# A four-layer graph network on one core: softmax sums one unit later, neighbour lists and weight products moved behind layer 0's first units

## The chip, the cores and the metric

The kernel runs on one core of a Trainium2 chip. The metric is the device time of one execution in microseconds. A core has five engines with instruction streams of their own: TensorE (PE; its weight loads are listed as PEld), VectorE (DVE), ScalarE (ACT), GpSimd (POOL) and SyncE (SP), which here only issues DMAs. The engines wait for one another by semaphores, and each runs its stream strictly in the order of the program.

## The reference

Four graph layers over 50,000 nodes with 256 features and 25,000 edges sorted by dst; after each a residual and a layer norm. Cut to what matters:

```python
def L0(x):   # dot-product weights without a maximum, sum over edges
    q, k, v = heads(x @ Wq), heads(x @ Wk), heads(x @ Wv)
    score = exp(clip(sum(k[src] * q[dst], -1) / sqrt(32), -5, 5))
    return segment_sum(v[src] * score, dst) / (segment_sum(score, dst) + 1e-9)
def L1(h):   # GIN
    z = (1 + eps) * h + segment_sum(h[src], dst)
    z = relu(z @ W1 + b1) @ W2 + b2
    return relu(layernorm(z + h) * gamma + beta)
def L2(x):   # GAT, with a self-loop for each node
    h = heads(x @ W); e = leaky_relu(a_src(h)[src] + a_dst(h)[dst])
    m = segment_max(e, dst); ex = exp(e - m[dst])
    alpha = ex / segment_sum(ex, dst)[dst]
    return layernorm(segment_sum(h[src] * alpha, dst) + bias + x) * ln_w + ln_b
def L3(x):   # attention with edge features
    k_j, v_j = (x @ Wk + bk)[src] + edge_attr @ We, (x @ Wv + bv)[src] + edge_attr @ We
    a = softmax over dst of sum(q[dst] * k_j, -1) / sqrt(32)
    return segment_sum(v_j * a, dst) + x @ Ws + bs
for L in (L0, L1, L2, L3):
    x = layernorm(x + L(x))
```

## The kernel before, in words

The nodes are worked in 196 units of 256 (two tiles of 128), the edges in 196 chunks of 128. Six stages run one after the other, each with a stream of its own on each engine: `prepare` (index lists, weights, constants; the first 55 us), `layer0` (to about 1045 us), `nodes1` (to 2470), `nodes2` (to 3610), `edges3` (to 4275) and `nodes3` (to the end).

Inside a stage the order is written by hand. `run_units(total, depth, body)` calls `body(s, at)` for steps s = 0, 1, 2, ..., once for each engine, and `at(lag)` is the unit s − lag, or none. So a job with lag 13 does in step s what belongs to unit s − 13, and the jobs of one step stand in each engine's stream in the order of the text. Steps of different engines are tied by semaphores alone.

**prepare.** SP and ACT load the two index arrays and the weights; DVE casts src and dst (L344, L346), makes three masks (L357 and behind it), a table of first edges (L372) that SP stores and loads again (L302, L304), then the products of weights and attention vectors (`wprod`, `watt`), the split of the biases into bf16 parts (`b3`, `b_sum`, L391) and their cast (L393).

**layer0.** POOL gathers source rows (L586), PE turns them (L627) and multiplies (L642); the messages go to memory and come back by SP (L504) for the sum over a unit's edges (L660). `pairs`, the neighbour lists that nodes1 to nodes3 use, is fetched by SP (L599, L601) in sixteen DMAs, eight of 16×24×256 integers (0.39 MB) and eight of 8×256, before SP's loads of unit 0.

**nodes2.** POOL gathers for each unit the rows of hh_d that its nodes' sources name (L1186, two DMAs a unit) into `near_rows`, a ring of NR = 16 buffers; it waits for the semaphore `weighed`. DVE multiplies them by the shares (`weighted`, L1403) and raises `weighed`. Shares are made for groups of GU = 8 units at once, on tiles of 128×128: scores turned by PE (L1241), maxima on DVE (tops), exp on ACT (L1499), sums on DVE (L1133, L1129, reciprocal L1393, shares L1411), turned back by PE (L1288, L1289) and copied as `own_first` by ACT (L1507). PE sums a unit's own shares into `own_ps` (L1297), DVE multiplies them by the unit's own rows (`own`, L1342), POOL adds the residual (L1193, semaphore `based`), and PE sums weighted rows, bias and own (L1265 to L1267) for the unit. PE's step begins with the transposes of L1250 and L1254. Other rings: `hot` of HOT buffers, `hin` of HR = 5, `xin` of XR = 9, `weighted` and `own` of WR = 4.

The lags that matter: POOL gathers at(0), adds own at(16); PE turns the shares and makes own_ps at(14), sums at(17); DVE maxima at(12), sums at(13), L1342 and L1403 at(15). POOL's body is:

```python
gp.wait_ge(weighed, u - NR + 1)     # unit at(0), then its two gathers
gp.indirect_dma_start(out=near_rows[:, u % NR, h, :], ...)
u = at(16)
gp.wait_ge(own_done, u + 1)         # then the own add of unit at(16)
gp.tensor_tensor(own..., own..., xin..., ALU.add).then_inc(based, 1)
```

**nodes3** has the same softmax without own shares: sums at(12), reciprocal at(13), shares at(14), the shares' transposes at(15) (L1785), product with the messages at(16) (L1718), sum at(18) (L1806); its messages come by SP into 24 buffers, and there are no gathers.

## Time and profile before

| | before |
|---|---|
| median of 3 runs | 5031.09 us |
| their lowest and highest | 5024.81, 5033.5 us |
| the profiled execution's own time | 4998.33 us |
| its span | 4996.6 us |
| busy PE, DVE, ACT, POOL | 91%, 80%, 56%, 50% |
| mean granted TensorE clock | 0.938 |

All rows come from the profiled execution, whose time lies 32.8 us below the median of the runs. A row of an instruction is: start in us, duration, engine, line of the kernel, operation, output<-inputs, shape; in brackets how long the engine stood idle before it and what ended that. A busy share over the whole span is a mean over six stages with limits of their own; each has to be read from its own windows.

### The profile page before, as it was taken

The numbers are of one execution on the slowest core, as the hardware profiler recorded it, in microseconds if no ns is written. First come the engines' busy times: TensorE is split into PE (matmuls) and PEld (weight loads), VectorE is DVE, ScalarE is ACT, GpSimd is POOL, SyncE is SP. The second block draws the span as 40 slices with busy tenths as digits, with TensorE's granted clock in tenths as the row PEclk, the third lists the DMA queues.
The fourth block names the chain that finished last, engine by engine and source line by source line (L and its number), as shares of the span: only waits on it lengthen the run. The fifth ranks groups of instructions, "written<-read, shape, count | busy, mean of one in ns | idle before, by whom it ended". The sixth has DMA issues, their size and how long they took to land. (4 is left out here: it accounts for less than half of the span.)

```text
span 4996.6 us, 90737 instructions
## 1 busy us (share of the span) xinstructions
PE 4563.9 (91%) x21673; PEld 3506.0 (70%) x21722; DVE 3986.5 (80%) x13147; ACT 2805.1 (56%) x6326; POOL 2476.3 (50%) x2462
## 2 busy tenths in 40 slices
PE   4999998779999999999888888888799999699998
PEld 3666664448888888888767777777566666577777
DVE  4777778979999999999859999999855555567666
ACT  1787886545555555555547777777611111366565
POOL 3555551237777777777466666666365554000000
PEclk8999996569999999999979999999899999899999
DMA  6777778954444444444468888787555554677775
GB/s 138 210 225 222 223 223 257 298 187 135 150 152 153 149 148 152 153 153 148 143 184 252 244 244 244 243 243 243 183 172 163 163 164 146 193 228 228 223 228 160
DMA packets 911233, 970.10 MB, mean 194 GB/s; under 512 B 104899, under 2 KB 867258, under 8 KB 910892
## 3 DMA queue, kind: packets, MB, share of 16 engines
q1 hardware_dynamic: 500692, 471.58, 32.9%
q10 hardware_dynamic: 327416, 315.35, 18.6%
q0 software_dynamic: 82784, 179.41, 12.3%
q8 instruction: 119, 1.95, 0.2%
q14 instruction: 222, 1.82, 0.1%
HBM read 654.56 MB, written 363.57 MB: 204 GB/s over the span
## 5 line engine op out<-in xcount | busy, mean ns | idle before, releaser
L1186 POOL DMA_INDIRECT nodes_near_rows<-hh_d,source_row x392 | 394.9, 1007 | 401.3 <-DVE nodes_weighted L1403 292.6
L586 POOL DMA_INDIRECT layer_xg<-in_x,edge_rows x392 | 386.7, 987 | 358.5 <-PE layer_t_ps L627 241.5
L884 POOL DMA_INDIRECT nodes_near_rows<-x_d,nodes_cur x392 | 419.0, 1069 | 238.2 <-POOL nodes_cur L879 170.8
L1542 POOL DMA_INDIRECT edges_xg<-x_d,edge_rows x392 | 372.9, 951 | 264.3 <-PE edges_x_ps L1568 172.6
L485 ACT ACTIVATE nodes_x<-nodes_outer_rows,nodes_outer_shift,nodes_outer_rstd 128x256 f32<-128x256 f32 x784 | 428.0, 597 | 61.1 <-issue 51.4
L1597 ACT ACTIVATE edges_xT<-edges_x_ps 128x512 f32<-128x512 f32 x196 | 117.1, 597 | 524.7 <-PE edges_x_ps L1568 524.7
L1806 PE MATMUL nodes_agg<-w_s,nodes_xT 128*128 128x256 f32 x1568 | 405.5, 381 | 0.0
L1004 PE MATMUL nodes_h_ps<-w_h,nodes_x2T 128*128 128x272 f32 x1568 | 392.2, 393 | 8.1 <-ACT nodes_x2T L1081 8.1
L660 PE MATMUL layer_agg<-layer_msg,layer_hot 128*128 128x264 f32 x784 | 314.2, 540 | 73.5 <-issue 65.7
L642 PE MATMUL layer_kv_ps<-w_kv,layer_xT 128*128 128x512 f32 x784 | 372.3, 597 | 1.0 <-DVE layer_made L751 1.0
L994 PE MATMUL nodes_out_ps<-w_b,nodes_hid 128*128 128x256 f32 x1568 | 371.2, 380 | 1.4 <-DVE nodes_inner_rows L925 0.8
L1014 PE MATMUL nodes_hid_ps<-nodes_zT,w_a 128*128 128x256 f32 x1568 | 370.5, 379 | 0.7 <-ACT nodes_zT L1088 0.7
L1633 DVE TENSOR_TENSOR edges_kv<-edges_kv_ps,edges_e_row 128x512 f32<-128x512 f32 x196 | 135.5, 692 | 295.2 <-PE edges_kv_ps L1584 295.2
L1584 PE MATMUL edges_kv_ps<-w_kv,edges_xT 128*128 128x512 f32 x784 | 368.4, 592 | 2.6
L660 PEld LDWEIGHTS layer_agg<-layer_msg,layer_hot 128*128 128x128 f32 x784 | 191.6, 260 | 219.3 <-issue 191.8
L1004 PEld LDWEIGHTS nodes_h_ps<-w_h,nodes_x2T 128*128 128x128 f32 x1568 | 297.3, 190 | 65.8 <-ACT nodes_x2T L1081 10.0
L899 POOL TENSOR_TENSOR nodes_x2b<-nodes_x,row_L_gnn_ln_b 128x512 f32<-128x512 f32 x196 | 265.8, 1356 | 142.0 <-DMA x_d<-nodes_x2b 131.4
L485 ACT ACTIVATE layer_y<-layer_ln_rows,layer_ln_shift,layer_ln_rstd 128x256 f32<-128x256 f32 x392 | 213.8, 592 | 217.0 <-DVE layer_ln_shift L478 217.0
L1014 PEld LDWEIGHTS nodes_hid_ps<-nodes_zT,w_a 128*128 128x128 f32 x1568 | 297.8, 190 | 46.5 <-ACT nodes_zT L1088 1.1
L1806 PEld LDWEIGHTS nodes_agg<-w_s,nodes_xT 128*128 128x128 f32 x1568 | 284.6, 191 | 31.0
L994 PEld LDWEIGHTS nodes_out_ps<-w_b,nodes_hid 128*128 128x128 f32 x1568 | 282.6, 190 | 32.4 <-issue 1.0
L941 DVE SCALAR_TENSOR_TENSOR nodes_scaled<-nodes_inner_rows,nodes_inner_moments,row_L_gnn_gamma 128x256 f32<-128x256 f32 x392 | 300.8, 806 | 0.0
(223 smaller groups left out, 12341.3 us busy)
## 6 DMA issues: line engine op xcount, KB each, us to landing
nodes_xin<-x_d SPq DMA_DIRECT2D x588, 256.0 KB, 3.8
layer_msg<-msg_d SPq DMA_DIRECT2D x392, 132.0 KB
hh_d<-nodes_hh ACTq DMA_DIRECT2D x196, 264.0 KB, 4.1
nodes_msg<-msg_d SPq DMA_DIRECT2D x392, 132.0 KB, 3.1
x_d<-layer_y ACTq DMA_DIRECT2D x196, 256.0 KB, 3.8
x_d<-nodes_x2b ACTq DMA_DIRECT2D x196, 256.0 KB, 3.5
nodes_hin<-hh_d SPq DMA_DIRECT2D x196, 256.0 KB, 3.9
x_d<-nodes_x ACTq DMA_DIRECT2D x196, 256.0 KB
```

The lines of the kernel that those rows point to most:

```text
L485: last = nc.scalar.activation(to[:, h, :], t["rows"][:, ring(u, 4), h, :], ACT.Identity, bias=t["shift"][:, ring(u, 4), h:h + 1], scale=t[ ...
L586: gp.indirect_dma_start(out=xg[:, c % 8, k, :], out_offset=None, in_=x, in_offset=bass.IndirectOffsetOnAxis(ap=edge_rows[:, c, k:k + 1], a ...
L642: last = nc.tensor.matmul(kv_ps[b][:, :], xT[:, b, 0, i, :], w0_kv[:, i, :], start=i == 0, stop=i == KC - 1)
L660: last = nc.tensor.matmul(agg[u % 2][:, h, 0:D + H], hot[:, u % 4, h, :], msg[:, r, h, :], start=True, stop=True)
L884: gp.indirect_dma_start(out=near_rows[:, r, h, :], out_offset=None, in_=x1_d, in_offset=bass.IndirectOffsetOnAxis(ap=cur[:, r, h:h + 1], a ...
L994: last = nc.tensor.matmul(out_ps[ring(u, 2)][:, h * D:(h + 1) * D], hid[:, ring(u, 2), k, h * P:(h + 1) * P], w1_b[:, k, :], start=k == 0, ...
L1004: last = nc.tensor.matmul(h_ps[:, h, 0:D + 2 * H], x2T[:, ring(u, 2), k, h, :], w2_h[:, k, :], start=k == 0, stop=k == KC - 1)
L1014: last = nc.tensor.matmul(hid_ps[:, m * 2 * P:(m + 1) * 2 * P], w1_a[:, k, m * P:(m + 1) * P], zT[:, ring(u, 2), k, :, :].rearrange("p h n ...
L1186: gp.indirect_dma_start(out=near_rows[:, u % NR, h, :], out_offset=None, in_=hh_d, in_offset=bass.IndirectOffsetOnAxis(ap=source_row[:, 2 ...
L1542: gp.indirect_dma_start(out=xg[:, c % 8, k, :], out_offset=None, in_=x3_d, in_offset=bass.IndirectOffsetOnAxis(ap=edge_rows[:, c, k:k + 1] ...
L1584: last = nc.tensor.matmul(kv_ps[r][:, :], xT[:, b, 0, j, :], w3_kv[:, j, :], start=False, stop=j == KC - 1)
L1806: nc.tensor.matmul(to, xT[:, u % 2, k, h, :], w3_s[:, k, :], start=k == 0, stop=False)
```

## The change

It has four parts.

In prepare, the casts of src stand behind the first mask. The loads of the attention vectors and of the biases (six DMAs), and all products of weights, leave prepare.

In layer0, ACT issues these six loads ahead of its first step, and DVE makes the products in twelve pieces, one a step, in steps U0 + 56 to U0 + 67. The masks of the lists, from step U0 + 6 on before, start at step U0 + 24. SP's sixteen `pairs` fetches stand two by two in units 8 to 15.

In nodes2 the sums stay where the maxima's group is one unit further on: sums at(14), the shares' transposes, own_first and own_ps at(15), L1342 and L1403 at(16), POOL's add at(17), PE's sum at(18), and everything behind it one step later; SP's loads of hin, attr and x move by one with them. HOT goes from 18 to 19. NR, XR, HR and WR stay.

In nodes3 the sums go to at(13), and all behind them one step later.

```diff
@@ prepare, DVE @@
-                for k in (1, 0):
-                    ve.wait_ge(edges_in[k], 48)
-                    nc.vector.tensor_copy(ends_f[:, k, :, :], ends_c[:, k, :, :]).then_inc(cast, 1)
-                for k in (1, 0):
-                    last = nc.vector.tensor_copy(pairs[:, :, :, k], ends_c[:, k, :, :])
-                last.then_inc(paired, 1)
+                ve.wait_ge(edges_in[1], 48)
+                nc.vector.tensor_copy(ends_f[:, 1, :, :], ends_c[:, 1, :, :]).then_inc(cast, 1)
+                nc.vector.tensor_copy(pairs[:, :, :, 1], ends_c[:, 1, :, :])
...
+                    if mask is below_lo:
+                        ve.wait_ge(edges_in[0], 48)
+                        nc.vector.tensor_copy(ends_f[:, 0, :, :], ends_c[:, 0, :, :]).then_inc(cast, 1)
+                        nc.vector.tensor_copy(pairs[:, :, :, 0], ends_c[:, 0, :, :]).then_inc(paired, 1)
@@ layer0 @@
-        MASKS = U0 + 6
+        MASKS, WEIGHTS = U0 + 24, U0 + 56
...
                 for u in range(UNITS):
+                    if 8 <= u < 8 + H:
+                        h = u - 8
+                        sp.wait_ge(lists_out, 16)
+                        sp.dma_start(pairs[h * 2 * GU:(h + 1) * 2 * GU, 0:WHOLE, :],
+                                     windows[0:WHOLE * 2 * GU, :].rearrange("(g w) x -> w g x", w=2 * GU)).then_inc(pairs_in, 16)
+                        sp.dma_start(pairs[h * REST:(h + 1) * REST, WHOLE, :], windows[WHOLE * 2 * GU:TILES, :]).then_inc(pairs_in, 16)
...
+                    if WEIGHTS <= s < WEIGHTS + 12:
+                        weights(s - WEIGHTS)
@@ nodes2 @@
-        NR, HR, XR, WR, HOT, LATER = 16, 5, 9, 4, 18, 12
+        NR, HR, XR, WR, HOT, LATER = 16, 5, 9, 4, 19, 12
...
-                    u = at(16)
+                    u = at(17)
                     if u is not None:
                         gp.wait_ge(own_done, u + 1)
...
```

How the streams stand, at the three places where instructions of different kinds change places:

POOL in nodes2, at the first own add (34 gathers stand ahead of it before, 36 after). Before:

```order
L1186 DMA nodes_near_rows<-hh_d,source_row 128x264
L1186 DMA nodes_near_rows<-hh_d,source_row 128x264 [waits nodes2_weighed]
L1186 DMA nodes_near_rows<-hh_d,source_row 128x264
L1193 TENSOR_TENSOR nodes_own<-nodes_own,nodes_xin 128x512 [waits layer0_made_out1,nodes2_own_done]
L1186 DMA nodes_near_rows<-hh_d,source_row 128x264 [waits nodes2_weighed]
```

and after:

```order
L1201 DMA nodes_near_rows<-hh_d,source_row 128x264 [waits nodes2_weighed]
L1201 DMA nodes_near_rows<-hh_d,source_row 128x264
L1201 DMA nodes_near_rows<-hh_d,source_row 128x264 [waits nodes2_weighed]
L1201 DMA nodes_near_rows<-hh_d,source_row 128x264
L1208 TENSOR_TENSOR nodes_own<-nodes_own,nodes_xin 128x512 [waits layer0_made_out0,nodes2_own_done]
L1201 DMA nodes_near_rows<-hh_d,source_row 128x264 [waits nodes2_weighed]
```

Two units' gathers that wait for `weighed`, instead of one's, stand ahead of the first add; from there on the two alternate unit by unit, as before. (A semaphore named for layer0 is one that nodes2 uses again for xin.)

SP at the start of layer0. `windows` are the lists, xin and msg are unit 0's loads. Before:

```order
L596 DMA windows<-layer_wrow 98x4x256
L599 DMA layer_pairs<-windows 16x24x256
L601 DMA layer_pairs<-windows 8x256
```

```order
L601 DMA layer_pairs<-windows 8x256
L495 DMA layer_xin<-in_x 128x2x256
L418 TENSOR_LOAD first_row
L418 ISA x16
L504 ISA
L504 DMA layer_msg<-msg_d 128x264
```

and after:

```order
L575 DMA windows<-layer_wrow 98x4x256
L467 DMA layer_xin<-in_x 128x2x256
L390 TENSOR_LOAD first_row
L390 ISA x16
L476 ISA
L476 DMA layer_msg<-msg_d 128x264
```

Between the two pieces of before stand the other seven pairs of fetches. After, unit 0's loads follow the lists directly.

DVE in nodes2, where the sums of a group begin (the scan of L1133, L1148 after). Before, behind the step with the maxima:

```order
L1388 TENSOR_TENSOR nodes_score_ps<-nodes_score_ps,nodes_top 128x256
L464 BN_AGGR nodes_inner_moments<-nodes_inner_parts 128x2 x2
L1403 TENSOR_TENSOR nodes_weighted<-nodes_near_rows,nodes_share_ps 128x512
L464 BN_AGGR nodes_outer_moments<-nodes_outer_parts 128x2 x2
L1422 TENSOR_TENSOR nodes_outer_rows<-nodes_agg,nodes_xin 128x512
L474 RECIPROCAL nodes_inner_rstd<-nodes_inner_dev 128x2
L474 RECIPROCAL nodes_outer_rstd<-nodes_outer_dev 128x2
L478 SCALAR_TENSOR_TENSOR nodes_inner_shift<-nodes_inner_moments,nodes_inner_rstd 128x2
L478 SCALAR_TENSOR_TENSOR nodes_outer_shift<-nodes_outer_moments,nodes_outer_rstd 128x2
L1133 SCALAR_TENSOR_TENSOR nodes_score_ps<-go_on,nodes_score_ps 128x128
```

and after:

```order
L430 BN_STATS nodes_outer_parts<-nodes_outer_rows 128x6 x2
L1396 TENSOR_TENSOR nodes_agg<-nodes_agg,row_L_gnn_ln_w 128x512
L436 BN_AGGR nodes_inner_moments<-nodes_inner_parts 128x2 x2
L1418 TENSOR_TENSOR nodes_weighted<-nodes_near_rows,nodes_share_ps 128x512
L436 BN_AGGR nodes_outer_moments<-nodes_outer_parts 128x2 x2
L1437 TENSOR_TENSOR nodes_outer_rows<-nodes_agg,nodes_xin 128x512
L446 RECIPROCAL nodes_inner_rstd<-nodes_inner_dev 128x2
L446 RECIPROCAL nodes_outer_rstd<-nodes_outer_dev 128x2
L450 SCALAR_TENSOR_TENSOR nodes_inner_shift<-nodes_inner_moments,nodes_inner_rstd 128x2
L450 SCALAR_TENSOR_TENSOR nodes_outer_shift<-nodes_outer_moments,nodes_outer_rstd 128x2
L1148 SCALAR_TENSOR_TENSOR nodes_score_ps<-go_on,nodes_score_ps 128x128
```

The step ahead of the sums is a plain one after the change; the maxima stand a step further up.

## Rows read from the trace of the kernel before

**Rows 1.** Windows: us, busy PE, PEld, DVE, ACT, POOL, granted clock, DMA share, GB/s
```profile
560.00:760.00 200.00, 200.00 (x783) 123.38 (x782) 141.70 (x557) 161.22 (x307) 108.43 (x109) 1.00 0.74 222
2800.00:3000.00 200.00, 178.20 (x1036) 150.42 (x1035) 185.19 (x661) 146.21 (x369) 122.59 (x112) 0.95 0.82 250
```
**Rows 2.** Line L1241 (count, ns, first and last start) and the waits, both from 2700 to 3500
```profile
L1241 PE MATMUL nodes_score_ps<-ident,nodes_att_edge x72: 275/275/275, 2728.4 to 3465.6; 128*128 128x128 f32 x72
```
```profile
POOL nodes_near_rows L1186 <- DVE nodes_weighted L1403: 240.7, 116, 4.1
```
**Rows 3.** Timeline of nodes2: the links of the loop
```profile
2552.65 0.59 PE L1297 MATMUL nodes_own_ps<-nodes_own_first,nodes_hot 128*128 128x8 f32 x4
2553.28 0.69 DVE L1342 SCALAR_TENSOR_TENSOR nodes_own<-nodes_own_ps,nodes_hin 128x512 f32<-128x512 f32 x1 [4.52 <-PE nodes_own_ps L1297]
...
2812.50 0.69 DVE L1342 SCALAR_TENSOR_TENSOR nodes_own<-nodes_own_ps,nodes_hin 128x512 f32<-128x512 f32 x1
...
2815.17 0.65 DVE L1403 TENSOR_TENSOR nodes_weighted<-nodes_near_rows,nodes_share_ps 128x512 f32<-128x512 f32 x1
...
2816.62 1.02 POOL L1186 DMA_INDIRECT nodes_near_rows<-hh_d,source_row  x1 [0.72 <-issue]
...
2818.97 1.29 POOL L1193 TENSOR_TENSOR nodes_own<-nodes_own,nodes_xin 128x512 f32<-128x512 f32 x1
2819.56 0.65 DVE L1403 TENSOR_TENSOR nodes_weighted<-nodes_near_rows,nodes_share_ps 128x512 f32<-128x512 f32 x1
...
2821.94 0.60 PE L1265 MATMUL nodes_agg<-nodes_weighted,nodes_hot 128*128 128x256 f32 x2
...
2825.12 0.59 PE L1297 MATMUL nodes_own_ps<-nodes_own_first,nodes_hot 128*128 128x8 f32 x4
```
**Rows 4.** Timeline of nodes2: the step with the sums, and the shares
```profile
2828.89 0.43 DVE L1133 TENSOR_TENSOR_SCAN nodes_score_ps<-go_on,nodes_score_ps 128x128 f32<-128x128 bf16 x1 [1.13 <-ACT nodes_score_ps L1499]
2829.23 0.67 DVE L1342 SCALAR_TENSOR_TENSOR nodes_own<-nodes_own_ps,nodes_hin 128x512 f32<-128x512 f32 x1
...
2833.20 0.65 DVE L1403 TENSOR_TENSOR nodes_weighted<-nodes_near_rows,nodes_share_ps 128x512 f32<-128x512 f32 x1
...
2840.62 0.61 PE L1297 MATMUL nodes_own_ps<-nodes_own_first,nodes_hot 128*128 128x8 f32 x4 [0.65 <-ACT nodes_own_first L1507]
```
**Rows 5.** PE's idle times and the clock behind them, timeline and windows
```profile
2834.02 0.64 PE L1250 MATMUL nodes_work_ps<-ident,nodes_hot 128*128 128x128 f32 x2 [2.61 <-ACT nodes_e_row L1489]
...
2877.32 1.19 PE L1265 MATMUL nodes_agg<-nodes_weighted,nodes_hot 128*128 128x256 f32 x2
...
2882.82 0.31 PE L1288 MATMUL nodes_share_ps<-ident,nodes_share 128*128 128x128 f32 x1
...
4401.23 0.30 PE L1785 MATMUL nodes_share_ps<-ident,nodes_share 128*128 128x128 f32 x1 [1.87 <-DVE nodes_weighted L1718]
```
```profile
4401.00:4403.00 2.00, 1.77 (x11) 1.59 (x12) 1.00 (x5) 0.98 (x3) 0.00 (x0) 1.00 0.58 193
2834.00:2836.00 2.00, 1.94 (x6) 1.32 (x7) 2.00 (x11) 1.12 (x3) 1.05 (x2) 0.53 0.64 219
```
**Rows 6.** Timeline of prepare and of layer0's first units
```profile
15.75 0.29 DVE L344 CAST prepare_ends_f<-prepare_ends_c 98x256 f32<-98x256 int32 x1 [7.22 <-DMA prepare_ends_c<-in_src]
15.96 0.49 DVE L346 COPY prepare_pairs<-prepare_ends_c 98x256 int32<-98x256 int32 x2
...
41.58 0.32 SPq L304 DMA_DIRECT2D first_col<-first_edges  x1
...
53.85 0.68 DVE L393 CAST bias<-prepare_b_sum 3x1024 bf16<-3x1024 f32 x1
...
81.09 6.63 SPq L601 DMA_DIRECT2D layer_pairs<-windows  x1
...
91.30 0.45 PE L627 MATMUL layer_t_ps<-ident,layer_xg 128*128 128x128 f32 x1 [4.08 <-issue]
...
121.36 0.78 PE L660 MATMUL layer_agg<-layer_msg,layer_hot 128*128 128x264 f32 x1 [7.88 <-DMA layer_msg<-msg_d]
```

177 lines of the change are left out of this document (90 added, 87 removed).

## The prediction

> **What bounds the kernel now.** I read the busy shares first, then the windows of the stages, then single rows. Layer 0's first half is bound by TensorE: 200.0 of 200 us busy at the full clock, while VectorE is busy 141.7 of 200 and the DMA engines 0.74 [rows 1]. In nodes2, the stage that the change rewrites most, two engines are close: VectorE 185.2 and TensorE 178.2 of 200 us [rows 1]. Its period is read from the score transposes of L1241, four to a group of eight units: 72 of them are 18 groups, the first at 2728.4 and the last at 3465.6, so a group takes (3465.6 − 2728.4)/17 = 43.36 us [rows 2]. A plain unit takes 4.39 us (VectorE's product of rows and shares, L1403, at 2815.17 and 2819.56 [rows 3]).
>
> The row that decided me is in the list of waits: POOL's gathers (L1186) wait for VectorE's L1403 of nodes2, 116 times in this stretch, 240.7 us in all [rows 2]. That wait is harmless today, because what POOL does next (its own add, L1193) is wanted late. The change makes it wanted early.
>
> **The change part by part. 1: the loop in nodes2.** near_rows has NR = 16 buffers. In step s POOL first issues the two gathers of unit s, which need the buffer of unit s−16, so they wait until L1403 has read it; the own add stands behind them. Before, VectorE weighs unit s−16 in its step s−1. After, the sums and all behind them are a step later, and NR stays: unit s−16 is weighed in VectorE's own step s. The own add of step s feeds TensorE's sums (L1265 to L1267) in step s+1; behind these, in order, stands L1297 of step s+1; VectorE's L1342 in step s+2 waits for that; and L1403 of step s+2 ends the round. So the ends of L1403 two steps apart are tied by one chain. Before, the same chain spanned three steps and did not bind. Its links, at full clock [rows 3]:
> - L1403's end, 2815.17 + 0.65 = 2815.82, to the first gather, 2816.62: 0.80.
> - First gather to the own add's end, 2818.97 + 1.29 = 2820.26: 3.64.
> - POOL to TensorE: no row shows this hop ended by L1193. The nearest is TensorE to VectorE, 2552.65 + 0.59 to 2553.28, 0.04; from above it is bounded by the 0.80 of the first link. I take 0.1, near the hop onto an engine that stood waiting with its operands ready.
> - L1265 (2821.94) to L1297 (2825.12): 3.18.
> - L1297 to L1342 where VectorE stood waiting for it: 2553.28 − 2552.65 = 0.63.
> - L1342 (2812.50) to L1403's end (2815.82): 3.32.
>
> The sum is 0.80 + 3.64 + 0.10 + 3.18 + 0.63 + 3.32 = 11.67 us for two steps, 5.83 a unit where a unit takes 4.39 now. It binds from POOL's step 17 to its last gathers in step 195: 179 steps, 22.4 groups. In each group there are extras on it. In the step with the sums L1342 to L1403's end is 2829.23 to 2833.85, 4.62 instead of 3.32: 1.30. The maxima have as much work, so 1.30 again. At the shares TensorE waits 0.65 for own_first ahead of L1297 [rows 4], and has the two transposes ahead of that, some 0.35: 1.0. Maxima, sums and shares now stand two steps from each other, on the same one of the two interleaved chains, so they add: 3.6. A group at full clock is 4 × 11.67 + 3.6 = 50.3 us.
>
> **2: the clock.** TensorE's work in a unit is some 3.9 us (178.2 of 200 us at 4.39 a unit, the groups' steps included), so per two steps it stands idle about 11.67 − 2 × 4.39 = 2.9 us beyond now, and in one piece: the delayed chain pushes the other until they are 4.39 apart, and 7.28 is left for the rest. What does a piece that long do? In each group of this stage there is one idle of 2.61 us, ahead of L1250 at 2834.02, and the 2 us behind it ran at a granted clock of 0.53, largely the lower level (1.2 GHz) [rows 5]. An idle of 1.87 us in nodes3 (L1785 at 4401.23) was followed by 1.00, the full 2.4 GHz [rows 5]. 2.9 is above 2.61, so I expect the drop in every pair. Its price: from L1265 at 2877.32 to L1288 at 2882.82, where L1297 would stand otherwise, is 5.50 us [rows 5] instead of 3.18, 2.32 more, with the whole stretch slow. If half of it is slow it is 1.2, and the transposes ahead of it, slow too, can add 0.6. I take 2.4 a pair: all of the stretch, and hardly anything for the transposes, which run beside POOL's gathers. The range is 1.7 to 2.9. The group is then 4 × (11.67 + 2.4) + 3.6 = 59.9 us, 16.5 above 43.36, and over 22.4 groups **+370 us**.
>
> The Trainium skill bears on this: "TensorE: Matmul & The Clock Gate", in Part 1, says that the throttled clock is the default and that activity releases it, and under "HAM oscillation" that repeated waits between short bursts of matmuls bring the low clock back each time. The rows of 2.61 us agree. Going by the row at 4401.23 alone one would say that the clock holds; that is the second case below.
>
> **3: the start.** In prepare the src casts no longer stand ahead of the masks. VectorE idled 7.22 us for the src load (L344 [rows 6]); it now runs on from dst, and meets src's two operations, 0.8 us with L346, behind the first mask: 6.4 us earlier. The weight products, up to 53.85 + 0.68 = 54.53, are gone, and SP's last load of the chain (issued 41.58) sets the end: 41.58 − 6.4 + about 2.3 of landing = 37.5 instead of 54.5, **−17.0**. The landing is an estimate from 1 to 4 us, so ±1.5.
>
> In layer 0 SP's sixteen fetches of pairs stood ahead of everything; one issue of them held SP 6.63 us [rows 6]. TensorE idled 4.08 us ahead of L627 (91.30) and 7.88 us ahead of unit 0's L660 (121.36), for messages that SP loaded late [rows 6]. Now the fetches come in units 8 to 15, and both waits should go. Each also let the clock fall, for which I put 5.6 us together (twice the 2.32 of the clock's price above is 4.6, and layer 0's matmuls are longer): **−17.6**. What comes in: the same eight times 0.4 MB, 3.2 MB, beside units 8 to 15. These are 56 us at 7 us each, so 57 GB/s; with the 222 of the row it is 279, where nodes2 moves 250 at a DMA share of 0.82 [rows 1]. It fits, if the queues share fairly; +1, with 0 to 8. ACT issues six loads ahead of its work, 2 us at SP's 0.32 for one at 41.58; its first job is not wanted until the first gathered chunk is in, so 0 to 2, I take 0. The weight products, some 13 us between 41.58 and 54.53, fall in twelve pieces on twelve steps of VectorE, which is idle 29% of 7 us, 2.0 us, in each [rows 1]; a piece may be three times the mean of 1.1, and then TensorE may wait 1 us for a step: +2, with 0 to 5. The start is −17.0 − 17.6 + 1 + 2 = **−32**, from −20 to −37.
>
> The Trainium skill ("Trainium Kernel Development and Optimization", Key Constraints) says that the DMAs of all queues run on the same 16 engines and interleave, so that moving an issue saves issue time only. By that the fetches' 3.2 MB would still cost what they cost, some 11 us at 279 GB/s, were DMA the bound. The share of 0.74 says that it is not.
>
> **4: nodes3.** The sums are a step later there too, with 24 message buffers, no gather and no own add. VectorE did not wait at its sums; TensorE waits 1.87 us a group at the shares for the last L1718 [rows 5], and both ends of that wait moved by one step. 0, with ±3.
>
> **The sum.** The profiled execution took 4998.3 us (its span 4996.6, 1.7 around it). 4998.3 + 370 − 32 = 5336. It lies 32.8 below the median of the three runs, 5031.1, so I add that: **5369**.
>
> **The rivals.** (a) The clock holds, as behind 1.87 us, because TensorE's transposes (L1250) run inside the wait and cut it in two. Then a group is 50.3: +6.9 × 22.4 = +155, and the time is 5031 + 155 − 32 = 5154. For it: L1250 stands ahead of L1265 in a step and is not held by POOL. Against it: L1250 runs directly behind L1297, so what is left is still one piece. (b) The clock drops in some pairs: 5200 to 5330. (c) Faster, as the change reads: the gathers' wait does not bind, because POOL runs ahead. This is decided where unit s−16 is weighed: if L1403 still ran a step before POOL's need. VectorE's wait of 1.13 us for exp at the sums [rows 4] then goes, and up to 0.9 more per group in the slow stretch: 0.9 to 2.0 × 24.5 groups = 22 to 49, with −32 about −67: 4964. Against it is that POOL already waits for this semaphore 116 times; it has no lead. (d) Clock low nearly throughout: TensorE's work of nearly the whole 4.39 us is doubled to 8.8 a unit, 70.4 a group, 27 above now, × 22.4 = 605: 5604.
>
> **How the numbers follow.** The forecast 0.62, (a) 0.18, (b) 0.08, (c) 0.08, (d) 0.04. What a measurement can tell from no change is about 0.2%, 10 us. Faster 0.08, the same 0.01, slower 0.91. The forecast's own range is 5280 to 5420 (clock price 1.7 to 2.9 a pair, start −20 to −37). With (a) and (b) it is 5130 to 5420; (c) and (d) are left out, 0.12.
>
> **What would show it.** In the profile after: POOL's own add followed by TensorE waiting at L1280 (L1265 before) for L1208 (L1193 before) in every second step; L1241's successors (L1256) 59.9 us a group apart, 50.3 by (a), 41.5 to 42.5 by (c); the granted clock of nodes2 well below 0.95; VectorE's busy share there below 75%; prepare ending near 37.5 us and no wait ahead of unit 0's L660. I am wrong if POOL is found to issue the gathers of unit s before VectorE's step s weighs, or if the idle comes as 1.5 us in each step instead of 2.9 in every second one.

## The result, and the profile after

| | before | after |
|---|---|---|
| median of 4 runs each | 5030.8 us | 5420.6 us |
| lowest and highest | 5024.8, 5033.5 | 5418.2, 5423.3 |
| profiled execution | 4998.3 us | 5422.3 us |
| mean granted clock | 0.938 | 0.910 |

The ratio is 1.0777, with a 95% interval from 1.0758 to 1.0795: the change makes the kernel 390 us slower. The forecast was 5369 us in a range from 5130 to 5420. Its direction and its cause were right; the measured median lies 0.6 us above the range and 51.6 us above the forecast. The profiled execution of before took 32.5 us less than the median of its runs, the one of after did not: the first experiment is on that.

The median says how much, not where. The line of the score transposes in nodes2 (L1256 after, L1241 in [rows 2]; count, durations in ns, first and last start) gives the period of a group of eight units:

```profile
L1256 PE MATMUL nodes_score_ps<-ident,nodes_att_edge x100: 272/275/421, 2528.6 to 3962.6; 128*128 128x128 f32 x96, 128*64 128x128 f32 x4
```
```profile
L1241 PE MATMUL nodes_score_ps<-ident,nodes_att_edge x100: 272/275/421, 2520.8 to 3549.7; 128*128 128x128 f32 x96, 128*64 128x128 f32 x4
```

The first fence is after, the second before over the whole stage. 100 of them are 25 groups, so 24 periods: (3962.6 − 2528.6)/24 = 59.75 us after, (3549.7 − 2520.8)/24 = 42.87 before. The forecast had 59.9 for a group. 24 × 16.88 = 405 us, more than the whole slowdown.

The windows of a stretch in the middle of nodes2 (the columns are those of [rows 1]; first after, then a second profile of the kernel before, told of below):

```profile
2812.00:3412.00 600.00, 437.69 (x2107) 353.07 (x2106) 378.07 (x1356) 299.78 (x755) 251.55 (x229) 0.82 0.58 170
```
```profile
2812.00:3412.00 600.00, 530.15 (x3032) 445.67 (x3031) 551.75 (x1953) 434.97 (x1088) 366.42 (x333) 0.94 0.81 246
```

No engine is full any more: VectorE fell from 92% to 63%, the DMA engines from 0.81 to 0.58, and TensorE's granted clock from 0.94 to 0.82. A stretch in which everything is idler and the work takes longer is a chain through several engines, not a busy engine. The timeline after shows it (start, duration, idle time and its end in brackets):

```profile
3010.41 1.19 PE L1280 MATMUL nodes_agg<-nodes_weighted,nodes_hot 128*128 128x256 f32 x2 [3.69 <-POOL nodes_own L1208]
...
3026.92 1.19 PE L1280 MATMUL nodes_agg<-nodes_weighted,nodes_hot 128*128 128x256 f32 x2 [3.24 <-POOL nodes_own L1208]
```
```profile
3006.69 1.02 POOL L1201 DMA_INDIRECT nodes_near_rows<-hh_d,source_row  x1 [7.41 <-DVE nodes_weighted L1418]
...
3009.04 1.27 POOL L1208 TENSOR_TENSOR nodes_own<-nodes_own,nodes_xin 128x512 f32<-128x512 f32 x1
3011.03 1.02 POOL L1201 DMA_INDIRECT nodes_near_rows<-hh_d,source_row  x1 [0.71 <-issue]
...
3023.19 1.02 POOL L1201 DMA_INDIRECT nodes_near_rows<-hh_d,source_row  x1 [8.54 <-DVE nodes_weighted L1418]
```

POOL works in pairs of steps: two units 4.34 us apart (3006.69 and 3011.03), then 12.16 us until the next pair (3023.19). TensorE waits 3.69 and 3.24 us for POOL's own add (L1208), which before never held it, and its first matmul behind the wait takes 1.19 us for two where it took 0.60 at the full clock [rows 3].

In the sum of stages the changed kernel stands like this. Each number is the distance between first or last starts of fixed lines: POOL's first gathers of each stage, layer0's first and last unit sum on PE, nodes2's first and last score transposes, nodes3's first share transposes, the end of the span. A plus sign in the last column is time lost. `before` is the profile that the prediction read, `before again` a second one, and `after` the changed kernel's.

| us | before | before again | after | after less before again |
|---|---|---|---|---|
| prepare, to layer0's first gather | 56.4 | 56.1 | 40.1 | −16.0 |
| from there to unit 0's sum | 65.0 | 69.8 | 65.0 | −4.8 |
| layer0's sums, first to last | 946.1 | 942.9 | 953.2 | +10.3 |
| to nodes2's first gather | 1426.0 | 1427.0 | 1427.9 | +0.9 |
| nodes2, to its first scores | 27.3 | 37.1 | 42.4 | +5.3 |
| nodes2, 24 groups | 1028.9 | 1029.1 | 1434.0 | +404.9 |
| nodes2, tail | 62.9 | 63.0 | 66.3 | +3.3 |
| edges3 | 672.9 | 688.8 | 687.4 | −1.4 |
| nodes3 | 711.1 | 709.8 | 704.2 | −5.6 |
| span | 4996.6 | 5023.6 | 5420.5 | +396.9 |

### The profile page after: what moved, and what is told of

Read it like the earlier page. It is cut to its first block and busy times, and to the rows that moved or that the text cites. A ratio compares the mean times of both kernels' runs of the same rounds, so it can differ in the third digit from the quotient of the medians.

```text
span 5420.5 us, 90743 instructions
## 1 busy us (share of the span) xinstructions
PE 4709.6 (87%) x21673; PEld 3594.5 (66%) x21722; DVE 3978.0 (73%) x13147; ACT 2799.7 (52%) x6324; POOL 2476.9 (46%) x2462
## 5 line engine op out<-in xcount | busy, mean ns | idle before, releaser
L1280 PE MATMUL nodes_agg<-nodes_weighted,nodes_hot 128*128 128x256 f32 x784 | 320.0, 499 | 298.7 <-POOL nodes_own L1208 162.8
L457 ACT ACTIVATE nodes_x<-nodes_outer_rows,nodes_outer_shift,nodes_outer_rstd 128x256 f32<-128x256 f32 x784 | 427.8, 597 | 59.9 <-issue 50.1
L1280 PEld LDWEIGHTS nodes_agg<-nodes_weighted,nodes_hot 128*128 128x128 f32 x784 | 172.6, 243 | 342.4 <-issue 175.3
L446 DVE RECIPROCAL nodes_outer_rstd<-nodes_outer_dev 128x2 f32<-128x2 f32 x392 | 58.6, 149 | 460.6 <-ACT nodes_outer_dev L441 458.7
```

Of the source, the lines that this page charges most:

```text
L457: last = nc.scalar.activation(to[:, h, :], t["rows"][:, ring(u, 4), h, :], ACT.Identity, bias=t["shift"][:, ring(u, 4), h:h + 1], scale=t[ ...
L1280: nc.tensor.matmul(cols, hot[:, u % HOT, h, :], weighted[:, u % WR, h, :], start=True, stop=False)
```

## The experiments

The kernels were timed in four sets, each on one chip and beside the kernel before; a ratio is always to the kernel before of the same set. Its median was 5029.0 us in the first set (c0, e2, e3, e6) and 5031.5 in the second (e4, e8, e1, e9), both on chip 9, 4999.6 in the third (e10, e12, e5, e13) on chip 0, and 5029.2 in the fourth (e14, e15) on chip 3.

### The kernel before, profiled again (c0)

> The kernel before, unchanged, profiled once more. Both kernels' profiled executions are known: 4998.3 us before (32.5 below its median of 5030.8) and 5422.3 after (at its median of 5420.6). Theory: the profiled execution of before happened to miss stalls at the starts of stages, of the kind that the profile after shows (ScalarE 7.1 and 8.5 us in layer0's start, 17.5 us in edges3's start, with hardly any DMA traffic), and a typical one has 30 us of them: the new profile lies near 5030 and shows one to three idles of 5 to 18 us on ScalarE, POOL and VectorE that no semaphore explains, in the first 60 us of layer0, nodes2 or edges3. Rival: the 32.5 us are spread over the whole span (steady parts slower by 0.65%): then the groups of nodes2 take 43.6 us instead of 43.36 and edges3's middle is slower too. Rival: stalls belong to the changed kernel's code alone: then this profile shows none and is near 4998.

The profiled run took 5025.3 us. The table above has its stages: 4.8 us more at the start of layer0, 9.8 at the start of nodes2, 15.9 in edges3, 30.5 us in all (the other stages give 3.5 back, and the spans differ by 27.0), and its groups take 42.88 us against 42.87. The windows of edges3's beginning, the first profile and then the second, at the same distance from the stage's first gather:

```profile
3632.00:3652.00 20.00, 19.89 (x80) 12.49 (x81) 10.95 (x27) 3.75 (x7) 15.40 (x16) 1.00 0.63 187
```
```profile
3644.00:3664.00 20.00, 7.45 (x19) 4.40 (x20) 5.38 (x13) 1.68 (x3) 11.25 (x12) 0.66 0.35 103
```

TensorE did 80 instructions in the one and 19 in the other. The list of waits of the second has, with releasers that the page can't name or that have nothing to do with the stage:

```profile
ACT layer_qs L694 <- remote: 9.9, 1, 9.9
```
```profile
ACT edges_xT L1597 <- DMA nodes_attr<-in_edge_attr: 16.9, 1, 16.9
```

So the theory holds, and both rivals fall: of the 32.8 us that the prediction added to its sum, 27 are found here, as idles at the starts of stages. They are in the kernel before too, and the profile that the prediction read had none. What ScalarE stands still for there was not found, and stays open.

### The wait alone, in the kernel before (e2)

```diff
-                            gp.wait_ge(weighed, u - NR + 1)
+                            gp.wait_ge(weighed, u - NR + 2)
```

> The kernel before with one edit: POOL's gathers of unit u in nodes2 wait for weighed to reach u - 14 instead of u - 15, the wait that the change brings; everything else as before. Theory (the loop through POOL, two steps long, with the clock dropping in every pair): a group of nodes2 takes about 60 us instead of 43.4, and the kernel is slower by 370 to 430 us, near 5430. Rival (the slowdown comes from the order of the sums and shares one unit later, or from DMA queues): this kernel stays within 30 us of 5031.

5365.9 us, ratio 1.0675 (1.0657 to 1.0692). One number in one wait, which orders nothing that needs ordering, costs 337 us. Its groups take 57.0 us in the mean. The rival is out: no sum was moved here. The theory's 370 to 430 was too much, by 2.75 us a group between 57.0 and 59.75, 66 us in all. The likely reason is where the extra work lies. The pairs of steps form two interleaved chains, one through the even and one through the odd steps. In this kernel maxima and sums lie in neighbouring steps, one on each chain, while in the changed kernel maxima, sums and shares all lie on the same one. The rows of this run fit that: on the chain with the maxima, L1403 starts at 2964.23, 2978.20, 2993.61, 3008.54 and 3022.51, so the four pairs of a group take 13.97, 15.41, 14.93 and 13.97 us, where the changed kernel's take 13.97, 15.41, 16.50 and 15.71 (shown further down). No run moves the maxima alone, so this is read from rows and not tested.

### POOL's add ahead of its gathers, in the changed kernel (e3)

```diff
                 def body(s, at):
+                    u = at(17)
+                    if u is not None:
+                        ...   # the own add
                     u = at(0)
                     if u is not None:
...                            # the two gathers
-                    u = at(17)
-                    if u is not None:
-                        ...   # the own add
```

> The changed kernel with POOL's own add of nodes2 put ahead of the two gathers in its step. The gathers still wait for the same semaphore value, but the own add no longer stands behind them, so the loop spans three steps again (11.7/3 = 3.9 us, below the 4.4 of a unit). Theory: the slowdown is gone whole; the time is 4970 to 5020, since the start (-9 to -32), nodes3 (-7) and the sums a unit later in nodes2 (0 to -49) remain. Rival: the slowdown is from the gathers' own lateness (their rows come late, whatever stands behind them): the time stays above 5300.

5033.3 us, ratio 1.0008 (0.9999 to 1.0018). The slowdown is gone with the same wait on the same semaphore in place, since nobody needs the gathers soon and somebody needs the add. POOL still waits for L1418, from 2700 to 3500 as much as it waited for L1403 before in the same window [rows 2]:

```profile
POOL nodes_near_rows L1206 <- DVE nodes_weighted L1418: 257.2, 123, 5.8
```

The expected 4970 to 5020 was not reached. A group takes 43.63 us, 0.75 more than before: the sums one unit later give nothing here, and what costs the 0.75 was not singled out. TensorE's idle of 2.61 us [rows 5] has become two of 1.86 and 1.38, and the clock falls all the same. The timeline of this kernel, and the window behind the first of the two:

```profile
2974.91 0.44 PE L1265 MATMUL nodes_work_ps<-ident,nodes_hot 128*128 128x128 f32 x2 [1.86 <-ACT nodes_e_row L1504]
2982.23 0.69 PE L1265 MATMUL nodes_work_ps<-ident,nodes_hot 128*128 128x128 f32 x2 [1.38 <-ACT nodes_e_row L1504]
```
```profile
2975.00:2980.00 5.00, 5.00 (x20) 3.93 (x20) 4.93 (x12) 2.64 (x6) 2.06 (x2) 0.66 0.46 146
```

### One more buffer, in the changed kernel (e1)

```diff
-        NR, HR, XR, WR, HOT, LATER = 16, 5, 9, 4, 19, 12
+        NR, HR, XR, WR, HOT, LATER = 17, 5, 8, 4, 19, 12
```

and the copy of the scores cut in two where a group wraps round the ring.

> The changed kernel with NR = 17 buffers for the gathered rows of nodes2 (XR = 8 instead of 9 makes the room; the copy of the scores is cut in two where a group wraps round the ring). The gathers of unit s then wait for unit s - 17, weighed a step earlier, as before the change; POOL's order is that of the changed kernel. Theory: the loop spans three steps again and the time is that of the kernel with the add ahead of the gathers, 5033, within 10 us. Rival (the wait for the ring is harmless and POOL's add itself is late, a step behind): stays above 5300. If XR = 8 binds, some 10 us more.

5039.3 us, ratio 1.0018 (1.0009 to 1.0028), groups of 43.75 us. The other way of breaking the loop gives the same time within 6 us (XR went from 9 to 8 with it), so it is the loop and not either of its links. Either repair leaves 43.6 to 43.8 us a group.

### Work added to TensorE, to keep its clock (e6, e8)

```diff
                     u = at(18)
                     if u is not None:
                         to = agg[u % 4]
+                        if u >= 4:
+                            pe.wait_ge(outer["filled"], u - 3)
+                        for k in range(6):
+                            nc.tensor.transpose(to[:, 0:P], ident[:, :], ident[:, :])
                         pe.wait_ge(weighed, u + 1)
                         pe.wait_ge(based, u + 1)
-                        if u >= 4:
-                            pe.wait_ge(outer["filled"], u - 3)
```

> The changed kernel with six extra transposes of the identity in each step of nodes2 on TensorE, into the bank that the unit's sum overwrites, ahead of the wait for POOL: 1176 instructions of pure extra work, about 1.3 us a step at full clock, inside TensorE's idle of 3.0 to 3.7 us in every second step. Theory (a low clock after each idle costs about 2.3 us in every pair of steps, and 6 us a group more around maxima and shares): the idles fall below 2.6 us, the clock holds in most pairs, and the kernel gets faster by 100 to 250 us in spite of the added work; granted clock of nodes2 from 0.82 to above 0.93. Rival (the loop's length is set by POOL and VectorE, and the clock costs nothing on it): same time within 20 us, or slower by up to 1.3 x 196 = 255 us where the extra work falls on the path.

5370.2 us, 50.4 less than the changed kernel's 5420.6, below what was expected. The timeline tells why: six transposes take 0.82 to 0.88 us, not 1.3, so too much of the idle was left. In one group (2984 to 3031) what was left in the four pairs was 2.91, 2.50, 1.74 and 1.37 us. Behind 2.91, 2.50 and 1.74 the clock was low (the two matmuls behind the idle take 1.11 to 1.19 us), behind 1.37 it held (0.67). In the next group an idle of 1.75 us was followed by the upper level:

```profile
3000.48 1.19 PE L1282 MATMUL nodes_agg<-nodes_weighted,nodes_hot 128*128 128x256 f32 x2 [2.50 <-POOL nodes_own L1208]
...
3015.95 1.11 PE L1282 MATMUL nodes_agg<-nodes_weighted,nodes_hot 128*128 128x256 f32 x2 [1.74 <-POOL nodes_own L1208]
...
3029.97 0.67 PE L1282 MATMUL nodes_agg<-nodes_weighted,nodes_hot 128*128 128x256 f32 x2 [1.37 <-POOL nodes_own L1208]
...
3076.97 0.67 PE L1282 MATMUL nodes_agg<-nodes_weighted,nodes_hot 128*128 128x256 f32 x2 [1.75 <-POOL nodes_own L1208]
```

So a larger dose, in the steps that wait for POOL alone (e8; the wait for `filled` stands ahead of it as in e6):

```diff
+                        if u % 2:
+                            for k in range(16):
+                                nc.tensor.transpose(to[:, 0:P], ident[:, :], ident[:, :])
```

> The changed kernel with sixteen extra transposes of the identity on TensorE in nodes2, in the steps of odd units alone, which are those that wait for POOL: 1568 instructions, about 2.4 us each time, inside idles of 3.0 to 3.7 us. Theory (the low clock after each idle costs 2.3 us in a pair): what is left of the idle is about 1 us, the clock stays at its upper level in nearly all of nodes2 (granted above 0.95 instead of 0.82), and a group falls from 59.8 to 50 to 52 us: faster than the changed kernel by 185 to 235 us, near 5210. Rival (clock costs little, as six transposes in each step brought 50 us only): within 60 us of 5420. Rival (the transposes themselves delay the sum's matmuls): slower than 5420.

5262.3 us, ratio to before 1.0459 (1.0443 to 1.0475): 158 us faster than the changed kernel, with 1568 useless instructions more. Groups of 52.7 us instead of 59.75, and the clock is back:

```profile
2812.00:3412.00 600.00, 505.44 (x3163) 433.17 (x3161) 442.39 (x1564) 346.62 (x875) 294.56 (x269) 0.97 0.67 198
```

The clock's rival is out, and so is the one by which the added work delays the sums. The Trainium skill ("TensorE: Matmul & The Clock Gate", "HAM oscillation") says that waits between short bursts of matmuls bring the low clock back each time; the trace agrees, with 0.82 granted where the waits are open and 0.97 where they are filled. The gain is 27 us short of the expected 185. The rows of one group show where the time goes, its plain pair first (L1421 is L1418 of the changed kernel, L1315 its L1312, L1360 its L1357, L1278 the fill):

```profile
3034.52 0.65 DVE L1421 TENSOR_TENSOR nodes_weighted<-nodes_near_rows,nodes_share_ps 128x512 f32<-128x512 f32 x1
3036.51 1.91 PE L1278 MATMUL nodes_agg<-ident 128*128 128x128 f32 x16
3039.74 0.67 PE L1283 MATMUL nodes_agg<-nodes_weighted,nodes_hot 128*128 128x256 f32 x2 [1.32 <-POOL nodes_own L1208]
3043.00 0.59 PE L1315 MATMUL nodes_own_ps<-nodes_own_first,nodes_hot 128*128 128x8 f32 x4
3043.18 0.23 ACT L1502 ACTIVATE nodes_att_edge<-nodes_work_ps 128x32 f32<-128x32 f32 x1 [3.60 <-PE nodes_work_ps L1295]
3043.87 0.17 DVE L446 RECIPROCAL nodes_outer_rstd<-nodes_outer_dev 128x2 f32<-128x2 f32 x1 [3.24 <-ACT nodes_outer_dev L441]
3044.27 0.68 DVE L1360 SCALAR_TENSOR_TENSOR nodes_own<-nodes_own_ps,nodes_hin 128x512 f32<-128x512 f32 x1
3046.93 0.65 DVE L1421 TENSOR_TENSOR nodes_weighted<-nodes_near_rows,nodes_share_ps 128x512 f32<-128x512 f32 x1
...
3060.74 0.65 DVE L1421 TENSOR_TENSOR nodes_weighted<-nodes_near_rows,nodes_share_ps 128x512 f32<-128x512 f32 x1
...
3074.67 0.66 DVE L1421 TENSOR_TENSOR nodes_weighted<-nodes_near_rows,nodes_share_ps 128x512 f32<-128x512 f32 x1
...
3087.53 0.66 DVE L1421 TENSOR_TENSOR nodes_weighted<-nodes_near_rows,nodes_share_ps 128x512 f32<-128x512 f32 x1
```

A plain pair takes 12.41 us with the clock held, where the forecast's sum at full clock was 11.67. The fill is not the cause: its sixteen transposes take 1.91 us, and TensorE stands idle for 1.32 us behind them before POOL's add is done. The difference is the link from TensorE's L1315 to VectorE's L1360, 1.27 us instead of 0.63. L1360 stands in VectorE's order behind L446, which waits for ScalarE's `outer_dev`; ScalarE made that at 3043.54 only, behind L1502, for which it had waited 3.60 us for TensorE.

### The parts without nodes2 (e4, e9, e12, e5)

The changed kernel with nodes2 as before (e4):

```diff
-    def nodes2(...)   # of the changed kernel
+    def nodes2(...)   # of the kernel before, NR 16 and HOT 18
```

> The changed kernel with nodes2 as it was before: only prepare, layer0 and nodes3 of the change. Theory (ledger of stages against the second profile of before: layer0's end and nodes1's start 9.6 us earlier, nodes3 5.6 us shorter, edges3 the same): 5029 - 15 = 5014 us, ratio 0.997, and nodes2's groups at 42.9 us. Rival (the prediction's sum for the start, -32, with nodes3 0): 4997. Rival (the 15 us in the ledger are scatter of single profiles): 5029.

5011.1 us, ratio 0.9962 (0.9948 to 0.9976): 20 us faster than before, so prepare, layer0 and nodes3 of the change are a gain. The theory's 5014 fits; the prediction's −32 gives 4999 here, and is too much.

The same with the weight products as 23 jobs, one a step (e9):

```diff
-                    if WEIGHTS <= s < WEIGHTS + 12:
-                        weights(s - WEIGHTS)
+                    if WEIGHTS <= s < WEIGHTS + len(jobs):
+                        jobs[s - WEIGHTS]()
```

> As e4_no_nodes2, but the weight products as 23 jobs of one or two instructions, one in each of 23 steps, instead of twelve pieces of up to 3.2 us of VectorE. Theory (in the profile after, the pieces cost 6 us: 72 matmuls of L622 in the 70 us from 525 instead of 78): 3 to 6 us faster than e4_no_nodes2, near 5010. Rival (the 6 us come from elsewhere, or VectorE has no room for them at any size): the same as e4_no_nodes2.

5010.5 us, ratio 0.9957 (0.9943 to 0.9970). The table's row for layer0's sums has 948.6 us here against 951.4 in e4, 2.8 less, which the times of the two kernels can't tell from nothing. The profiles of all runs together can: this row is 942.9 to 946.2 us in the four profiles in which layer0 is that of before (before, before again, e2, e5), 951.4 to 956.1 in the seven with the twelve pieces (after, e15, e3, e1, e6, e8, e4), and 947.7 to 950.5 in the four with 23 jobs (e9, e14, e10, e13). So the finer jobs cost about half of what the twelve pieces cost. That the twelve pieces cost TensorE time is plain in the profile after too: 248 instructions in the 70 us from 560, where the kernel before does 275.

```profile
560.00:630.00 70.00, 64.77 (x248) 38.94 (x248) 53.62 (x189) 51.42 (x98) 37.14 (x36) 1.00 0.68 203
```
```profile
560.00:630.00 70.00, 70.00 (x275) 43.22 (x274) 49.50 (x197) 56.01 (x107) 38.91 (x40) 1.00 0.73 221
```

The fetches of the neighbour lists alone, in the kernel before (e12):

> The kernel before with the fetches of the neighbour lists moved behind the first units (two in each of units 8 to 15), and the masks started at step U0 + 24, nothing else. The prediction put 17.6 us on this, less 1 for the fetches' new place. Theory now (the waits that it removes, 4.1 and 7.9 us, go, but an idle of ScalarE of 7 to 10 us with no DMA traffic takes their place): 3 to 9 us faster than before, near 5025. Rival (as predicted): 16 us faster, near 5014.

The edit moves the sixteen fetches into units 8 to 15 and sets `MASKS = U0 + 24`. 4985.8 us against 4999.6, ratio 0.9973 (0.9963 to 0.9983): 14 us, much nearer the prediction's 16.6 than the new theory's 3 to 9. The profiles of this set have none of the idles in layer0's and edges3's start that cost so much in c0. In e12's own profile unit 0's sum comes 50.7 us after the first gather, against 64.4 in e5, which has layer0 as before, and layer0's sums take 946.0 us, no more than the 945.1 of e5. So the fetches cost hardly anything in their new place. The rule of the Trainium skill that the prediction weighed ("Trainium Kernel Development and Optimization", Key Constraints: all queues share the 16 engines) put no price on them here; the share was 0.74 [rows 1].

nodes3 of the change alone, in the kernel before (e5):

> The kernel before with nodes3 of the change alone. The prediction said 0, with 3 either way. Theory now, from the two profiles (5.6 us less from the first share transposes to the end): 5 to 7 us faster, near 5024. Rival: 0, the 5.6 us being scatter of one profile.

4991.1 us against 4999.6, ratio 0.9984 (0.9975 to 0.9993): 8.5 us faster, where the prediction had 0. TensorE's wait at the shares, over the whole stage, is 45.0 us before and 38.9 in e5 (39.2 in the changed kernel), which is most of what the stage gains: from the first share transposes to the end it takes 703.9 us in e5 and 711.1 in the profile of before.

```profile
PE nodes_share_ps L1785 <- DVE nodes_weighted L1718: 45.0, 24, 2.1
```
```profile
PE nodes_share_ps L1785 <- DVE nodes_weighted L1718: 38.9, 24, 1.6
```

### Two fills that went wrong (e10, e13)

Twelve transposes once a group in e9, whose nodes2 is that of before, ahead of the step behind the sums (e10); and the whole change with POOL's add first, the finer weight products, and eight transposes in two steps of each group (e13). The edit of e10:

```diff
+                        c = at(14)
+                        if c is not None and c % GU == 0:
+                            v = at(17)
+                            if v is not None and v >= 4:
+                                pe.wait_ge(outer["filled"], v - 3)
+                            for _ in range(12):
+                                nc.tensor.transpose(agg[...][:, 0:P], ident[:, :], ident[:, :])
                         if k >= 1:
                             pe.wait_ge(e_copied, k)
```

> e9_fine (prepare, layer0 and nodes3 of the change, nodes2 as before) with twelve extra transposes of the identity on TensorE in nodes2, once a group, ahead of the transposes of L1265 that stand idle 2.61 us behind the sums. Theory (an idle that long drops the clock and the two steps behind it are slow): a group goes from 42.9 us to 41 to 42, 20 to 45 us faster than 5010, the granted clock of nodes2 from 0.94 to above 0.97. Rival (VectorE, busy 92% there, sets the group's length): same as e9_fine within 8 us, whatever the clock.

> The whole change with the two repairs found so far (POOL's own add ahead of its gathers, weight products one or two instructions a step) and eight extra transposes in each of the two steps of a group whose first transposes stand idle 1.86 and 1.38 us, so that the clock holds. With the add first alone the change was at 5033, its groups at 43.6 us against 42.9 before, and low clock behind these idles. Theory (the sums a unit later do remove VectorE's wait for exp, and the low clock hides the gain): groups of 41 to 42 us, 4980 to 5000. Rival (the later sums lengthen the chain through VectorE and give nothing at any clock): groups stay at 43.4 to 43.7, near 5025.

e10 gave 4991.8 us (ratio 0.9984, 0.9975 to 0.9993) with groups of 43.80 us, and e13 5031.8 us (1.0063, 1.0049 to 1.0077) with groups of 45.45. Both are slower in nodes2 than without the fill, against 42.9 and 43.6. In e10 the wait that the fill needs for its bank stands ahead of the step's transposes, where before it stood behind them, and TensorE now idles 3.62 us for VectorE's outer rows ahead of it. The low level comes during or behind the fill all the same: in the row below the twelve transposes take 2.82 us, where sixteen took 1.91 at the upper level in e8. Over the window from 2812 to 3412 the granted clock of e10 is 0.96 against 0.93 in e9, and the groups are longer even so:

```profile
2984.47 2.82 PE L1265 MATMUL nodes_agg<-ident 128*128 128x128 f32 x12 [3.62 <-DVE nodes_outer_rows L1443]
```

So neither says what the low clock costs in nodes2 without the loop, nor what the later sums are worth with the clock held; both stay open.

### Once more, for the start (e14, e15)

> e9_fine once more. In two calls the kernel before took 5029 and 5031.5 us and its stages began with idles that no semaphore explains; in a third it took 4999.6 and had none, like the profile that the prediction was read from. Theory: the start of layer0 is worth 17 us where those idles are absent and 5 us where they are present, so the ratio to before is 0.9957 again if before is near 5030, and 0.992 to 0.993 (4960 to 4966 us) if before is near 5000. Rival: the gain is the same 20 us on either.

> The changed kernel once more, to read its stages beside a kernel before of the same call. Theory: nodes2 costs 405 us in its 24 group periods wherever it runs; if before is near 5030, the time is 5420 and the ratio 1.0777 again; if before is near 5000, the stages' starts lose 30 us and layer0's start gains what was forecast: 5370 to 5385, near the forecast's 5369 less its 32.8 for the median. Rival: the slowdown scales with the chip and the ratio is 1.0777 in both.

This set was like the first two: before 5029.2 us, e14 5009.2 (ratio 0.9953, 0.9939 to 0.9966), the changed kernel 5416.3 (1.0772, 1.0755 to 1.0788). Both repeat. Since the other condition did not come again, the changed kernel was not timed in it. What is known of the start there comes from the third set: from the first gather to unit 0's sum it is 47.8 us in e10 and 50.4 in e13, which have layer0 of the change, and 50.7 in e12, against 65.0 in the prediction's profile of before and 64.4 in e5. That is 14 to 17 us less, where the prediction took 17.6. In the other sets the same distance is 65.1 in e4 against 69.8 in before again, 5 less.

## Why the prediction was right, and where it was wrong

**The loop was right, and so was its form.** The forecast said that POOL's add would stand behind gathers that wait for the same step, and that the steps would come in pairs with one idle that drops the clock. Moving the wait alone makes the kernel 337 us slower, breaking the chain at either of two links takes the slowdown away, and with the clock held the kernel is 158 us faster. Case (a), the clock holds, case (b), it drops in some pairs only, and case (c), the wait doesn't bind, are out: all four pairs of the group below carry the low clock. Of the points that would show it, VectorE below 75% and the lower clock came as said. TensorE waits for POOL's add in all four pairs of a group, starting L1280 0.10 us after L1208's end as forecast, though the profile names L1208 in two of them only. 59.75 us a group is the mean over 24 periods; in the middle of the stage the period is 61.9.

**The step that failed: the length of the round at full clock, in its link from L1297 to L1342.** The forecast put 0.63 us on this link. Rows of the changed kernel, over one group (L1312 and L1357 are the two ends of the link now):

```profile
2989.83 0.66 DVE L1418 TENSOR_TENSOR nodes_weighted<-nodes_near_rows,nodes_share_ps 128x512 f32<-128x512 f32 x1
...
3005.24 0.65 DVE L1418 TENSOR_TENSOR nodes_weighted<-nodes_near_rows,nodes_share_ps 128x512 f32<-128x512 f32 x1
...
3016.29 0.59 PE L1312 MATMUL nodes_own_ps<-nodes_own_first,nodes_hot 128*128 128x8 f32 x4
3017.77 0.68 DVE L1357 SCALAR_TENSOR_TENSOR nodes_own<-nodes_own_ps,nodes_hin 128x512 f32<-128x512 f32 x1
3021.74 0.66 DVE L1418 TENSOR_TENSOR nodes_weighted<-nodes_near_rows,nodes_share_ps 128x512 f32<-128x512 f32 x1
...
3034.12 0.61 PE L1312 MATMUL nodes_own_ps<-nodes_own_first,nodes_hot 128*128 128x8 f32 x4 [0.65 <-ACT nodes_own_first L1522]
3037.45 0.65 DVE L1418 TENSOR_TENSOR nodes_weighted<-nodes_near_rows,nodes_share_ps 128x512 f32<-128x512 f32 x1
...
3042.63 0.80 PE L1280 MATMUL nodes_agg<-nodes_weighted,nodes_hot 128*128 128x256 f32 x2 [3.02 <-issue]
3047.57 0.59 PE L1312 MATMUL nodes_own_ps<-nodes_own_first,nodes_hot 128*128 128x8 f32 x4
3048.44 0.17 DVE L446 RECIPROCAL nodes_outer_rstd<-nodes_outer_dev 128x2 f32<-128x2 f32 x1 [4.88 <-ACT nodes_outer_dev L441]
3048.75 0.69 DVE L1357 SCALAR_TENSOR_TENSOR nodes_own<-nodes_own_ps,nodes_hin 128x512 f32<-128x512 f32 x1
3051.42 0.65 DVE L1418 TENSOR_TENSOR nodes_weighted<-nodes_near_rows,nodes_share_ps 128x512 f32<-128x512 f32 x1
```

The starts of L1418 give the four pairs of steps. Beside them stand the same pairs with the clock held (e8, the starts of L1421) and the forecast:

| us | forecast, full clock | e8, clock held | after |
|---|---|---|---|
| pair with the maxima | 12.97 | 13.81 | 15.41 |
| pair with the sums | 12.97 | 13.93 | 16.50 |
| pair with the shares | 12.67 | 12.86 | 15.71 |
| plain pair | 11.67 | 12.41 | 13.97 |
| group | 50.3 | 53.0 | 61.6 |

At full clock a plain pair is 0.74 us longer than the sum of links, and nearly all of it is this link: 1.27 us in e8, and 1.18 to 1.48 in three pairs of four after. The forecast had read 0.63 at 2553.28 [rows 3], near the start of the stage, where no norm of an earlier unit is worked yet (the first `outer_rstd` comes at 2575.1). Later on L1342 stands in VectorE's order behind `outer_rstd`, and that waits for ScalarE. So a second path, from TensorE through ScalarE to VectorE, ends the link. This is read from the rows; no run took that wait out. In the pair with the shares the link is 0.65 as forecast, since own_first is later still.

The extras of maxima, sums and shares are 3.4 us a group at full clock (53.0 − 4 × 12.41), where the forecast had 3.6. The clock costs 8.6 us a group (61.6 − 53.0) where it had 4 × 2.4 = 9.6, but spread otherwise: 1.56 in a plain pair, 1.6 with the maxima, 2.6 with the sums and 2.9 with the shares, whose transposes and copy run at the low clock too. That a plain pair took 13.97 us after, beside the forecast's 11.67 + 2.4 = 14.07, is therefore luck in part: a round too short and a clock too dear made up for each other there, and did not in the other pairs. In sum a group is 61.6 in these rows, 61.9 in the mean of the 18 periods from 2742 to 3856, and 59.9 in the forecast. So a bound group costs 18.5 us over the 43.4 of before instead of 16.5, and the 24 groups 405 instead of 370: 35 of the 51.6 us.

The tail of nodes2, which the forecast left out, lost 3.3 us more. The 5.3 at its start are not the change's: with nodes2 as before that row of the table is 37.1 to 42.4 us in the sets near 5030 (before again, e2, e4, e9, e14), and 42.4 after.

**A reading that was off without harm.** The prediction gave TensorE 3.9 us of work a unit, from 178.2 of 200 us and the 4.39 of a plain unit. With the groups' steps a unit lasts 43.36/8 = 5.42 us, and TensorE works 4.8 of them. Only case (d) leaned on it.

**The start was half wrong.** Prepare gave 16.0 us (17.0 forecast). Layer0's start gave 4.8 instead of 17.6 in the condition in which the times were measured, since idles of ScalarE of 7.1 and 8.5 us took the place of the waits removed, and 14 to 17 in the condition of the profile that was read. Layer0's sums took 10.3 us more than in the shortest profile of before, where products and fetches were put at 3. The fetches were priced right (+1; e12 shows next to nothing). The products in twelve pieces, put at 2, cost some 8: 951.4 to 956.1 us against 942.9 to 946.2. Why a piece of up to three instructions holds TensorE, although VectorE is idle 29% of the time in the mean, was not found; that cutting the pieces halves the cost speaks for their length. Together −9.6 instead of −32, 22.4 us.

**nodes3** gave 5.6 to 8.5 us instead of 0: the two ends of TensorE's wait at the shares did not move alike, and it shrank by 6 us in all.

**The base.** The 32.8 us between the profiled execution and the median were taken as a constant. Most of them are idles at the starts of stages. For the changed kernel, whose profile shows them itself, the sum against `before again` is: 338 forecast, + 43.5 for nodes2, + 22.4 for the start, − 5.6 for nodes3, − 1.4 for edges3, gives 396.9, the difference of the spans. The medians differ by 389.8 us, 7 less; a single profile lies a few us from the median of its runs.

**The range** was added up wrongly at its upper end. With the clock at 2.9 us a pair a group is 4 × 14.57 + 3.6 = 61.9, so 22.4 groups add 415 us, and with the start at −20 the time is 5031.1 + 415 − 20 = 5426, not 5420. It held no width for the links of the round, the term that failed, and the clock's upper price would have covered for it.

**What came out.** The version with the lowest ratio is the change without its nodes2 (e4), with or without the finer pieces (e9, e14): 0.9953 to 0.9962 of the time before. Beside the fetches (14 us) and nodes3 (8.5 us) it holds the shorter prepare. The sums one unit later in nodes2 gave nothing in any version tried; with POOL's add first a group takes 43.6 us against 42.9 before.

## What to carry to other kernels

When one job is moved a step later in a software pipeline, every ring of buffers that ends in this job has lost a step; look on each engine for what stands behind the wait that guards the ring, and count how many steps the shortest chain through it now spans. A wait that is long in the profile and harmless tells only that what follows it is not yet needed, and ordering the urgent job ahead of the patient one costs nothing where a bigger ring costs memory. A link that is read where the stage has just started can be too short: look for its length in the middle of the stage, with all that stands ahead of it in the stream. And extras that fall on a loop have to be priced at the clock in which the loop runs.

## What the runs showed of the hardware

Chips, or the conditions in which they were found, differ by 30 us in this kernel: the kernel before took 5029.0 and 5031.5 us on chip 9 and 5029.2 on chip 3 (9 to 15 runs each), and 4999.6 on chip 0 (25 runs, 4996.2 to 5004.2). The profiles at 5030 us have idles of 4 to 21 us on ScalarE, VectorE and POOL in the first 60 us of layer0 and edges3, and a slower start of nodes2. The groups of nodes2 agree within 0.1%, layer0's sums within 0.4%. What the idles are is not known.

Useless matmuls in an idle of some 3 us made the kernel 158 us faster, by the granted clock: 0.82 without and 0.97 with them.

The length of a single idle doesn't decide whether the clock falls. In e6 an idle of 1.74 us was followed by the lower level and one of 1.75 us, in the same place of the next group, by the upper. In e3 an idle of 1.86 us was followed by 0.66 in the next 5 us, while one of 1.87 us in nodes3 was followed by 1.00 [rows 5]. The idles of 2.6 us in the kernel before and of 3.2 to 3.7 us in the changed one were followed by the lower level in the rows read; but in e8 one of 3.10 us, behind the fill, was followed by the upper:

```profile
3386.70 0.67 PE L1283 MATMUL nodes_agg<-nodes_weighted,nodes_hot 128*128 128x256 f32 x2 [3.10 <-POOL nodes_own L1208]
```
```profile
3386.70:3388.70 2.00, 2.00 (x10) 1.63 (x11) 0.17 (x1) 0.30 (x2) 1.68 (x2) 1.00 0.11 17
```
